# Attention over four levels: queries and keys in two fp32r pieces, two heads in the halves of the array

## What is computed

```
def _mha(x, w_in, b_in, w_out, b_out):
    qkv = x @ w_in.T + b_in
    q, k, v = jnp.split(qkv, 3, axis=-1)
    split = lambda t: t.reshape(B, S, H, hd).transpose(0, 2, 1, 3)
    scores = jnp.einsum('bhqd,bhkd->bhqk', q, k) / jnp.sqrt(jnp.asarray(hd, x.dtype))
    attn = jax.nn.softmax(scores, axis=-1)
    out = jnp.einsum('bhqk,bhkd->bhqd', attn, v)
    return out.transpose(0, 2, 1, 3).reshape(B, S, E) @ w_out.T + b_out
for lvl in range(4):                       # 1024, 512, 256, 128 tokens
    outs.append(_mha(query[:, ::2 ** lvl, :], in_proj_w[lvl], ...))
# from the coarsest level: linear upsampling to the finer one, @ up_w[lvl].T + up_b[lvl], + outs[lvl]
x = _layernorm(x + current)
h = silu((x @ w1.T) * w1_s) * ((x @ w2.T) * w2_s)
h = gelu((h @ h1.T) * h1_s);  h = gelu((h @ h2.T) * h2_s)
x = _layernorm(x + (h @ w3.T) * w3_s)
```

## Time and profile before

| | us |
|---|---|
| median of 3 runs | 4299.57 |
| lowest, highest | 4291.9, 4299.97 |
| the profiled execution's own time | 4300.24 |
| span of its profile | 4298.4 |
| TensorE matmuls busy | 3855.2 |
| VectorE busy | 2566.8 |
| ScalarE busy | 2483.7 |
| GpSimd busy | 1211.1 |

### The profile page before, as it was taken

The page is one execution under the profiler, slowest core; times in us unless marked ns, Lnnn a source line. Parts: engine busy times, 40 slices in busy tenths (PEclk is TensorE's granted clock), DMA queues, the critical chain, the costliest instruction groups (busy, mean ns, idle before and its releaser), DMA issues. The chain is left out here.

```text
span 4298.4 us, 69980 instructions
## 1 busy us (share of the span) xinstructions
PE 3855.2 (90%) x20881; PEld 2139.9 (50%) x20881; DVE 2566.8 (60%) x4681; ACT 2483.7 (58%) x3261; POOL 1211.1 (28%) x1144
## 2 busy tenths in 40 slices
PE   4589999989989999999999999918999999999998
PEld 2233334334333433333333333206887877877887
DVE  2377787787787787787787788643333333333333
...
PEclk6699999999999999999999999958999999999999
...
DMA packets 308845, 307.48 MB, mean 72 GB/s; under 512 B 75169, under 2 KB 285281, under 8 KB 308193
## 3 DMA queue, kind: packets, MB, share of 16 engines
...
...
## 5 line engine op out<-in xcount | busy, mean ns | idle before, releaser
L760 ACT ACTIVATE a_probs<-a_p_s 128x1024 f32<-128x1024 f32 x1360 | 1322.4, 1020 | 610.4 <-PE a_p_s L1000 603.2
L839 DVE TENSOR_REDUCE a_part_max<-a_p_m 128x1 f32<-128x512 f32 x2048 | 1338.5, 680 | 434.6 <-PE a_p_m L1015 429.7
L1015 PE MATMUL a_p_m<-a_k_st,a_q_st 96*128 96x512 bf16 (+2 forms) x2944 | 1010.3, 375 | 184.5 <-DVE a_part_max L839 85.4
L1395 PE MATMUL p_h<-f_h_hi,f_w_hi 128*128 128x512 f32 x2048 | 809.9, 395 | 40.0 <-issue 35.2
L1000 PE MATMUL a_p_s<-a_q_st,a_k_st 98*128 98x512 bf16 (+2 forms) x2944 | 822.2, 367 | 11.0 <-DMA a_q_st<-a_neg_bf 6.8
L1395 PE MATMUL p_h<-f_h_lo,f_w_hi 128*128 128x512 f32 x2048 | 806.3, 394 | 1.6 <-issue 1.6
L1015 PEld LDWEIGHTS a_p_m<-a_k_st,a_q_st 96*128 96x128 bf16 x2944 | 258.7, 97 | 1085.2 <-DVE a_part_max L839 692.0
L1032 PE MATMUL a_p_o<-a_probs,a_v_aug 128*17 128x512 f32 (+2 forms) x5888 | 729.3, 575 | 0.8 <-ACT a_probs L760 0.8
L1364 DVE TENSOR_TENSOR f_h_lo<-f_h_f,f_h_hi 128x512 fp32r<-128x512 f32 x256 | 177.1, 692 | 720.3 <-ACT f_h_hi L1277 720.3
L839 DVE TENSOR_REDUCE a_row_max<-a_p_m 128x1 f32<-128x512 f32 (+2 forms) x672 | 439.9, 680 | 176.3 <-PE a_p_m L1015 171.6
L1275 ACT ACTIVATE f_h_f<-p_h,f_sc 128x512 f32<-128x512 f32 x256 | 176.6, 690 | 583.2 <-PE p_h L1395 583.1
...
## 6 DMA issues: line engine op xcount, KB each, us to landing
...
```

Of the source, the lines that this page charges most:

```text
L760: act.activation(probs[:, s % 2, 2 * p:2 * p + 2, :], p_s[:, 2 * p:2 * p + 2, :], ACT.Exp, scale=HD ** -0.5).then_inc(exp_done.sem, 1)
L839: dve.reduce_max(out, src, AX.X).then_inc(max_read.sem, 1)
L1015: ins = pe.matmul(p_m[:, n % 2, r * size:(r + 1) * size], q_st[0:ROWS, unit.place, j, q * 128:(q + 1) * 128], k_st[0:ROWS, unit.halves[kb] ...
L1395: ins = pe.matmul(out, a, c, start=first and n == 0, stop=last and n == len(terms) - 1)
```

## The change

Queries, keys and negated maxima become two fp32r pieces each instead of three (maxima two) bf16 ones; three products of pieces are kept instead of six, 48 rows, 50 with the maxima. The four blocks of a unit lie as two pairs: one of a pair in partitions 0 to 49, the other in 64 to 113. A matmul of L1000 or L1015 so uses 64 rows of the array, at row position 0 or 64 (`HALF`), with 128 columns; the order within a step is m0 low, m1 high, m2 low, scores high then low, m3 high, scores low then high. `BANK_HEAD` and `max_column` name the heads accordingly. GpSimd has one operation for a projection instead of three, and `qk` is gone: ScalarE writes straight into `qk_cut`, and waits ahead of that for the stores of two projections before. `neg_cut` is one buffer where `neg_bf` was two, so ScalarE's neg task of unit n waits for the DMAs of unit n-1; they are four instead of two. The stack DMAs stay 12 (two halves by three pieces by two), each with half the heads in four-byte numbers; scratch is 2 x 4 bytes a number instead of 3 x 2. `timeline` is as it was. The core of the diff:

```diff
 DH = 1024
 EPS = 1e-5
-K_PIECES = (0, 0, 0, 1, 1, 2)
-Q_PIECES = (0, 1, 2, 0, 1, 0)
+K_PIECES = (0, 0, 1)
+Q_PIECES = (0, 1, 0)
+HALF = 64
...
         x_hi, x_lo = sb("x_hi", [128, 2, S0], F32R), sb("x_lo", [128, 2, S0], F32R)
-        qk = sb("qk", [128, W])
-        qk_bf = sb("qk_bf", [128, 2, 3, W], BF16)
-        k_st = sb("k_st", [128, HALVES, HG, W], BF16)
-        q_st = sb("q_st", [128, HALVES, HG, W], BF16)
+        qk_cut = sb("qk_cut", [128, 2, 2, W], F32R)
+        k_st = sb("k_st", [128, HALVES, HG // 2, W], F32R)
+        q_st = sb("q_st", [128, HALVES, HG // 2, W], F32R)
...
-        neg_f = sb("neg_f", [HG, W])
-        neg_bf = sb("neg_bf", [HG, 2, 2, W], BF16)
+        neg_cut = sb("neg_cut", [HG, 2, W], F32R)
...
-                                    src = scr[lvl][t, pieces[r], unit.head * 16:(unit.head + heads) * 16, :]
-                                    dst = st[16 * r:16 * r + 16, unit.halves[0]:unit.halves[0] + len(unit.halves), :, :]
-                                    if lvl == 0:
-                                        src = src.rearrange("(h d) (b t) -> d b h t", d=16, b=2)
...
+                                    rows_of = scr[lvl][t, pieces[r], unit.head * 16:(unit.head + heads) * 16, :]
+                                    for e in range(2):
+                                        at = HALF * e + 16 * r
+                                        dst = st[at:at + 16, unit.halves[0]:unit.halves[0] + len(unit.halves), :, :].bitcast(F32)
+                                        src = rows_of[heads * 8 * e:heads * 8 * (e + 1), :]
+                                        if lvl == 0:
+                                            src = src.rearrange("(s d) (b t) -> d b s t", d=16, b=2)
...
+                                        sp.dma_start(dst, src).then_inc(stacked[n].sem, 16)
                         elif kind == "neg":
                             place = UNITS[n].place
                             sp.wait_ge(neg_b.sem, neg_b.value(it, n + 1))
                             hold()
-                            for i in range(2):
-                                sp.dma_start(q_st[ROWS + i:ROWS + i + 1, place, :, :],
-                                             neg_bf[0:HG, n % 2, i, :]).then_inc(neg_placed[n % 2].sem, 16)
+                            for e in range(2):
+                                for i in range(2):
+                                    at = HALF * e + ROWS + i
+                                    sp.dma_start(q_st[at:at + 1, place, :, :].bitcast(F32),
+                                                 neg_cut[2 * e:2 * e + 2, i, :].bitcast(F32)).then_inc(neg_placed[n % 2].sem, 16)
...
@@ -638,20 +649,13 @@
                                 .then_inc(o_lo_done.sem, 1)
                         elif kind == "proj":
                             size = min(W, tokens(PROJ[n][0].lvl)) * len(PROJ[n])
-                            bf, rest = qk_bf[:, n % 2, :, 0:size], qk[:, 0:size]
+                            hi, lo = qk_cut[:, n % 2, 0, 0:size], qk_cut[:, n % 2, 1, 0:size]
                             pool.wait_ge(qk_hi.sem, qk_hi.value(it, n + 1))
-                            pool.tensor_tensor(out=rest, in0=rest, in1=bf[:, 0, :], op=ALU.subtract)\
-                                .then_inc(qk_rest_done.sem, 1)
-                            pool.wait_ge(qk_rest_done.sem, qk_rest_done.value(it, n + 1))
-                            pool.sem_inc(held.sem, 1)
-                            pool.tensor_copy(bf[:, 1, :], rest).then_inc(qk_b.sem, 1)
-                            pool.wait_ge(qk_b.sem, qk_b.value(it, n + 1))
-                            pool.tensor_tensor(out=bf[:, 2, :], in0=rest, in1=bf[:, 1, :], op=ALU.subtract)\
-                                .then_inc(qk_c.sem, 1)
+                            pool.tensor_tensor(out=lo, in0=lo.bitcast(F32), in1=hi, op=ALU.subtract).then_inc(qk_c.sem, 1)
...
@@ -737,22 +741,20 @@
                             lvl = PROJ[n][0].lvl
                             size = min(W, tokens(lvl))
                             act.wait_ge(qk_mm.sem, qk_mm.value(it, n + 1))
-                            qk_c.wait(act, it, n)
+                            stored[n % 2].wait(act, it, STORED[n] - len(PROJ[n]))
                             for i, (_, t, m, blk) in enumerate(PROJ[n]):
                                 part = slice(i * size, (i + 1) * size)
-                                ins = act.activation(qk[:, part], p_a[:, part], ACT.Identity, bias=col[:, lvl, CQK + 2 * t + m:CQK + 2 * t + m + 1])
+                                ins = act.activation(qk_cut[:, n % 2, 1, part].bitcast(F32), p_a[:, part], ACT.Identity, bias=col[:, lvl, CQK + 2 * t + m:CQK + 2 * t + m + 1])
                             ins.then_inc(qk_read.sem, 1)
                             act.wait_ge(qk_read.sem, qk_read.value(it, n + 1))
-                            stored[n % 2].wait(act, it, STORED[n] - len(PROJ[n]))
                             every = slice(0, len(PROJ[n]) * size)
-                            act.activation(qk_bf[:, n % 2, 0, every], qk[:, every], ACT.Copy).then_inc(qk_hi.sem, 1)
+                            act.activation(qk_cut[:, n % 2, 0, every], qk_cut[:, n % 2, 1, every].bitcast(F32), ACT.Copy).then_inc(qk_hi.sem, 1)
                         elif kind == "neg":
                             act.wait_ge(neg_mm.sem, neg_mm.value(it, n + 1))
-                            neg_b.wait(act, it, n)
-                            neg_placed[n % 2].wait(act, it, n // 2)
-                            act.activation(neg_f[:, :], p_a[0:HG, 0:W], ACT.Copy, scale=-1.0).then_inc(neg_read.sem, 1)
+                            neg_placed[(n - 1) % 2 if n else 0].wait(act, it, (n + 1) // 2)
+                            act.activation(neg_cut[:, 1, :].bitcast(F32), p_a[0:HG, 0:W], ACT.Copy, scale=-1.0).then_inc(neg_read.sem, 1)
                             act.wait_ge(neg_read.sem, neg_read.value(it, n + 1))
-                            act.activation(neg_bf[:, n % 2, 0, :], neg_f[:, :], ACT.Copy).then_inc(neg_hi.sem, 1)
+                            act.activation(neg_cut[:, 0, :], neg_cut[:, 1, :].bitcast(F32), ACT.Copy).then_inc(neg_hi.sem, 1)
...
@@ -994,11 +1006,12 @@
                             if kt == 0 and p == 0:
                                 neg_placed[u % 2].wait(pe, it, u // 2 + 1)
                             exp_done.wait(pe, it, n - 1)
-                            for j in (2 * p, 2 * p + 1):
+                            for j in ((1, 0), (2, 3))[p]:
+                                low = HALF * (j % 2)
                                 for i in range(parts):
                                     half, key = divmod(i * size + kt * 128, W)
-                                    ins = pe.matmul(p_s[:, j, i * size:(i + 1) * size], k_st[0:ROWS + 2, unit.halves[half], j, key:key + 128],
-                                                    q_st[0:ROWS + 2, unit.place, j, i * size:(i + 1) * size], start=True, stop=True)
+                                    ins = pe.matmul(p_s[:, j, i * size:(i + 1) * size], k_st[low:low + ROWS + 2, unit.halves[half], p, key:key + 128],
+                                                    q_st[low:low + ROWS + 2, unit.place, p, i * size:(i + 1) * size], start=True, stop=True)
                             ins.then_inc(score_mm.sem, 1)
                         elif kind == "max":
                             u, m = MAX_OF[n]
@@ -1006,14 +1019,15 @@
                             parts, blocks = across(unit.lvl), len(unit.halves)
                             size = W // parts
                             if m == 0 and u == STACKS[STACK_OF[u]][0]:
-                                stacked[STACK_OF[u]].wait(pe, it, 2 * len(K_PIECES))
+                                stacked[STACK_OF[u]].wait(pe, it, 4 * len(K_PIECES))
                             max_read.wait(pe, it, n - 1)
+                            low = HALF * (m % 2)
                             for r in range(parts):
-                                head, kb = divmod(m * parts + r, blocks)
-                                q, j = divmod(head, HG)
+                                turn, kb = divmod(m // 2 * parts + r, blocks)
+                                q, pair = divmod(turn, 2)
                                 key = q * 128 // size * size if parts > 1 else 0
-                                ins = pe.matmul(p_m[:, n % 2, r * size:(r + 1) * size], q_st[0:ROWS, unit.place, j, q * 128:(q + 1) * 128],
-                                                k_st[0:ROWS, unit.halves[kb], j, key:key + size], start=True, stop=True)
+                                ins = pe.matmul(p_m[:, n % 2, r * size:(r + 1) * size], q_st[low:low + ROWS, unit.place, pair, q * 128:(q + 1) * 128],
+                                                k_st[low:low + ROWS, unit.halves[kb], pair, key:key + size], start=True, stop=True)
                             ins.then_inc(max_mm.sem, 1)
```

(2 more changed lines are left out.)

55 lines of the change are left out of this document (34 added, 21 removed).

## The result

| | before | changed |
|---|---|---|
| median of 4 runs, us | 4299.58 | 4401.05 |
| lowest, highest | 4291.9, 4299.97 | 4397.19, 4419.21 |
| span of the profiled execution | 4298.4 | 4397.6 |

The ratio is 1.0252, with a 95% interval of 1.0228 to 1.0276: +101 us where +36 was forecast. The page after shows where to look first. Its clock row answers to the earlier trace rows; the weight loads answer to the earlier trace rows.

What follows compares the result with a forecast made beforehand. Plain attention steps were taken as bound by a ring through VectorE and TensorE, side steps by TensorE itself. 62 + 11 - 57 + 8 + 7 + 5 = +36 us gave 4336 us; likeliest case 4290 to 4385, whole range 4210 to 4480.

Steps and rivals of the forecast that it cites:

- Plain steps, +62: Attention steps without side work or four transposes: two waiting weight loads cost more, +0.22 us in each of 280 steps.
- The ring: Cycle through VectorE's reads of maxima, maximum 1, value product and maximum 2, said to set the plain step's 3.13 us.
- Transposes, +11: Attention steps with four small transposes: 3.26 us becomes 3.35, 0.09 more in each of 120 steps.
- Side steps, -57: Attention steps with projection matmuls, bound by TensorE: halves side by side save 0.22 us in each of 260 steps.
- The rival of free layout changes: Switching TensorE between halves and whole array costs nothing, side steps take 3.54 to 3.75 us; 4234 us, chance 0.25.
- Narrow matmuls, +8: Two coarsest levels of attention: matmuls of 32 or 64 columns meet the 0.118 us floor for a weight load.
- Halves not side by side (4593): Rival: matmuls in opposite array halves run one after another, side steps take 4.85 us; 4593 us, chance 0.15.
- The maxima's wait: ScalarE stands 3.9 us per batch element for the negated maxima's DMAs; some 0.9 reaches TensorE, +7 us in all.
- Part 2: One buffer for negated maxima and four DMAs: +7 us for ScalarE's waits, +5 in the opening, stack loads 0.
- the clock rival: TensorE, standing some 35% of a plain step, drops to the lower clock there; over 4570 us, chance 0.05.

Runs made afterwards that it cites:

- e3_bf16: The changed kernel with its score and maximum matmuls reading the high two bytes of each fp32r number as bf16; 4303.8 us.
- e9_onehalf: The kernel before with three bf16 products instead of six, 48 rows (50 with the maxima), all in one half of the array; 4606.5 us.
- e6_store: The changed kernel with the stores of a projection 0.9 of a step earlier in SyncE's queue; 4381.2 us.
- e1_fill: The changed kernel with the four score matmuls of each of the 35 steps without side work issued twice; 4351.5 us.

## Why the prediction was wrong

**The sum without the clock held roughly.** It had +36; the trace has -11 in the steps, +11 in the opening and +3 behind, with the clock taken out +3.
- *Plain steps, +62.* The ring was right, its step 3.29, not 3.35: the two uncovered loads cost 0.10 each, as e3_bf16 shows, but from the read of maximum 2 to the load of maximum 1 it is 1.34 (1090.06 to 1091.40), where two reads and the 0.05 behind them made 1.39. By the count there are 237 such steps and not 280; most grew by 0.15 to 0.21 at full clock, but one in each element, in place 68, shrank from 5.50 to 3.87, so all together came to about +20.
- *Transposes, +11:* +10, but near by luck: most grew by 0.02 to 0.04 (0.09 forecast), and the sum comes from three places of an element (+0.2, +0.3 and +0.7).
- *Side steps, -57:* -45. Median of maximum 2 to last score 1.10 to 0.80, maximum 0 to V 0.54 to 0.45, V to maximum 2 as it was; against it the entry to the projection +0.22 and the way out +0.09 (means 0.36 to 0.59, 0.17 to 0.26). I had +0.40 for both and a shorter block. (The prediction's remark that these steps keep half of what the halves save is a slip by its own figures: 0.22 of 0.61 is a good third.) The change of layout costs about 0.3 in a round trip, and the load under it nothing more. The rival of free layout changes falls with that. The Trainium skill, TensorEngine Tiling (Array Packing), section Key Properties, says that changing the tiling mode drains TensorE; the +0.22 and +0.09 agree with it.
- *Narrow matmuls, +8:* the coarse and boundary steps came to +4 at full clock.
- *Halves not side by side (4593):* out, by the starts at 1089.53. e9_onehalf is that case in bf16, and measured 4606, near this number by luck: its side steps are 4.52 and not 4.85, its plain ones 3.12, and the rest is 618 us at the lower clock.

**The maxima's wait was there, the stores' wait I had not priced.** ScalarE stood 2 to 3 us once an element for the maxima's DMAs, 3.9 forecast. What reached TensorE of it was not measured. But the prediction's Part 2 never costs the store wait that now stands ahead of ScalarE's first operation of a projection. It was 62.9 us of standing, and 20 to 28 us of the time by e6_store.

**The step that failed is the clock rival.** It stood at 0.05, it looked only at plain steps, and it asked only how long TensorE stands. The clock fell to the lower level for 287 us more, mostly in the coarse units and at the ends of units, and this cost about 96 us (the estimate above), all of what the sum missed and more. What should have raised it is in the diff: 96 rows of the array become twice 48, used side by side in part of the time only. The runs show that the rows a matmul uses move the granted clock: with the whole array 112, 96, 80 and 66 rows gave 65, 65, 90 and 423 us at the lower level, in one half 62 and 48 rows gave 420 and 618, side by side 62 and 48 rows gave 184 and 352. In the changed kernel itself the zero rows take back 168 of the 287 us, so rows account for over half of the added lower level; the rest is not separated.

The Trainium skill, TensorE: Matmul & The Clock Gate, section What's actually happening, says that the clock is set by how busy TensorE has been. The fall at 1221 does come behind a stretch in which TensorE stood in part (3.51 of 5.20 us busy). But the same steps at full clock, with TensorE no less busy in them, had 65 us at the lower level with 96 rows and 423 us with 66, so here the rows belong to it as well. More matmuls help too (e1_fill). How rows and time weigh against each other stays open.
